# Order within a step: transposes ahead of the values of the job two back, high halves ahead of the outputs

## The chip, the cores and the metric

The kernel runs on one core of one Trainium2 chip. The metric is the device time of one execution in microseconds (us), on that one core. A core has a matrix engine (TensorE, PE in the profile, with its weight loads as PEld), VectorE (DVE), ScalarE (ACT), GpSimd (POOL) and a queue that issues DMAs (SyncE, SP). Each engine works through its own list of instructions in the order in which it was written. Engines wait for each other only by semaphores.

## The reference, cut to what matters

The input x is 4 sequences of 1024 rows of 1024 numbers. The block is a causal attention with 16 heads of 64 over a context, followed by one linear layer. Both have a layer norm ahead and a residual behind.

```
def attention(q, k, v):                      # per head, D = 64, SCALE = D ** -0.5
    scores = einsum('qd,kd->qk', q, k) * SCALE
    scores = where(key > query, -inf, scores)
    p = exp(scores - scores.max(-1))
    return (p / p.sum(-1)) @ v

x = x + attention(layernorm(x), ctx, ctx)
weight = einsum('oin,n->oi', sigmoid(pweight) - sigmoid(nweight), exps * sigmoid(mask_weight)) * scale
bias = bit_ste(einsum('on,n->o', pbias - nbias, bexps)) * biasscale
x = x + layernorm(x) @ weight.T + bias
```

## The kernel before, in words

The 4096 rows are 32 **tiles** of 128 rows, eight to a sequence. Tile t is number i = t mod 8 in its sequence and sees i + 1 blocks of 128 keys. The heads of a tile are cut into **jobs**: four heads to a job at i = 0 and 1, two at i = 2 and 3, one at i = 4 to 7. A tile so has 4, 4, 8, 8, 16, 16, 16 and 16 jobs, 352 in all. One job is one **step** of the main loop on every engine. A job with heads x (i + 1) blocks has 4 to 8 blocks.

What happens to job j, and where:

- **Scores** (PE, lines 395 to 419): queries times keys in two fp16 terms, and the causal mask as one more matmul, into `slot`, a PSUM buffer with two places (one per parity of j). They are issued in step j - 2, and wait until the exponentials of job j - 2 have freed the place.
- **Maxima** (DVE, line 647) and **exponentials** (ACT, line 533, each followed by a short read of the row sums), also in step j - 2. They leave the probabilities in fp32 in `p32`.
- **Transposes** (PE, line 427), step j: each block of probabilities is transposed in fp32 into `ptb`, a PSUM buffer with two places of four blocks. A job of 5 to 8 blocks fills both places, as chunk 0 and chunk 1. A chunk waits until the low half of the chunk two back has been taken from its place (`lo_done`, line 425).
- **High halves** (ACT, line 549), step j: each chunk is scaled and copied as fp16 to `pt`, after `t_done` of the chunk. Ahead of the first chunk ACT waits for `pv_done` of job j - 2 (line 546), since those values read the same place of `pt`.
- **Low halves** (DVE, line 653), step j: fp32 minus the high half, as fp16.
- **Values** (PE, lines 431 to 450), issued two steps later, in step j + 2: transposed probabilities times values, into `oacc`, the one PSUM buffer for the outputs of a group of four heads. The first job of a group waits until the output of the group before has been taken (`osb_done`).
- **Output** (ACT, line 556): when the values of a group's last job are done, ACT copies `oacc` to `osb`, in the step in which those values run. POOL adds it to the residual.

In the tiles of 8 and 16 steps, jobs q = 3, 6, 9, ... of tile 4 and later (92 jobs) are **turned by DMA** instead: ACT copies the high half of the untransposed probabilities (line 542), DVE makes the low half (line 661), and a DMA transposes both (`pd<-pd`, line 318). Such a job has no transposes, high halves or low halves in its own step. It has values, which wait for the DMA (`pt_in`).

The **linear** layer of an earlier tile is spread over the steps (line 464): 3 matmuls per step in a 16-step tile, 6 in an 8-step tile, 12 in a 4-step tile. The conversions of queries, context and y (lines 565, 573, 580) go at fixed steps. In a 16-step tile they stand at the end of steps 8, 4 and 0 on ACT. In the first 16 steps of the kernel the weights are also made (lines 488, 589, 594, 714, 718 and 885), and in the steps of jobs 4 and 5 the bias (`bias_part`). The linear layer of the last three tiles runs after the last job.

The order of the work is written out by hand in the loop of each engine (line 506 for PE, 616 for ACT, 772 for DVE). A step of PE was: scores of j + 2, values of j - 2, transposes of j, [weights, bias], linear. A step of ACT was: output, high halves of j, exponentials of j + 2 and the copy of a turned job, conversions. A step of DVE is: maxima of j + 2, low half of the turned job j + 1, reciprocals, low halves of j.

## Time and profile before

| what | value |
|---|---|
| median of 3 runs | 1213.82 us (1211.16 to 1218.65) |
| the profiled execution's own time | 1213.7 us |
| its span in the trace | 1211.9 us |
| busy PE, PEld | 1109.8 us, 803.6 us |
| busy DVE, ACT, POOL | 968.1 us, 922.2 us, 687.4 us |
| granted TensorE clock, mean | 0.982 |

Busy time is the sum of an engine's instructions. Matmuls overlap in the pipeline, so the length of one matmul's row is more than the time from its start to the next start. The length of a stage on PE is therefore read from the start of its first matmul to the start of the next stage's first matmul. The time that an engine stood idle ahead of an instruction stands in brackets behind the row, with what ended it.

### The profile page before, as it was taken

The numbers are of one execution on the slowest core, as the hardware profiler recorded it, in microseconds if no ns is written. First come the engines' busy times: TensorE is split into PE (matmuls) and PEld (weight loads), VectorE is DVE, ScalarE is ACT, GpSimd is POOL, SyncE is SP. The second block draws the span as 40 slices with busy tenths as digits, with TensorE's granted clock in tenths as the row PEclk, the third lists the DMA queues.
The fourth block names the chain that finished last, engine by engine and source line by source line (L and its number), as shares of the span: only waits on it lengthen the run. The fifth ranks groups of instructions, "written<-read, shape, count | busy, mean of one in ns | idle before, by whom it ended". The sixth has DMA issues, their size and how long they took to land. (4 is left out here: it accounts for less than half of the span.)

```text
span 1211.9 us, 28076 instructions
## 1 busy us (share of the span) xinstructions
PE 1109.8 (92%) x10788; PEld 803.6 (66%) x10788; DVE 968.1 (80%) x1424; ACT 922.2 (76%) x1898; POOL 687.4 (57%) x766
## 2 busy tenths in 40 slices
PE   4787889899999999889999999999999999899988
PEld 3676756566666776666766777676776676677753
DVE  5756677888888887888888887888888788888862
ACT  6899866688787787677787787788788787787750
POOL 3465546554446886454446986555348986463251
PEclk8889898999999999999999999999999999999999
DMA  9999726575759786675759886764658986654442
GB/s 317 287 321 330 256 71 118 129 148 108 150 121 175 178 186 130 140 141 106 151 120 201 150 191 128 159 158 107 127 119 199 183 173 143 135 105 97 86 88 70
DMA packets 382581, 190.88 MB, mean 158 GB/s; under 512 B 358128, under 2 KB 358128, under 8 KB 378352
## 3 DMA queue, kind: packets, MB, share of 16 engines
q1 hardware_dynamic: 381440, 189.05, 68.1%
q8 instruction: 86, 1.41, 0.5%
q14 instruction: 47, 0.39, 0.1%
q10 hardware_dynamic: 1008, 0.04, 0.1%
HBM read 67.15 MB, written 16.78 MB: 69 GB/s over the span
## 5 line engine op out<-in xcount | busy, mean ns | idle before, releaser
L533 ACT ACTIVATE p<-slot,mx 128x512 f32<-128x512 f32 (+7 forms) x512 | 378.0, 748 | 142.8 <-DVE mx L647 89.9
L647 DVE TENSOR_REDUCE mx<-slot 128x1 f32<-128x640 f32 (+7 forms) x352 | 356.8, 1016 | 32.4 <-PE slot L417 30.5
L464 PE MATMUL ffnb<-wt,yt 128*128 128x512 f16 x1464 | 373.0, 381 | 3.1 <-DVE ring L709 1.7
L653 DVE SCALAR_TENSOR_TENSOR pt<-ptb,pt 128x512 f16<-128x512 f32 (+1 forms) x504 | 281.9, 599 | 102.7 <-ACT pt L549 102.3
L413 PE MATMUL slot<-kt,qt 128*128 128x128 f16 (+3 forms) x1056 | 268.6, 284 | 16.4 <-ACT p L533 10.9
L414 PE MATMUL slot<-kt,qs 128*128 128x128 f16 (+3 forms) x1056 | 268.2, 284 | 0.0
L549 ACT ACTIVATE pt<-ptb 128x512 f16<-128x512 f32 (+1 forms) x504 | 239.9, 528 | 30.4 <-PE ptb L427 28.1
L427 PE MATMUL ptb<-id,p 128*128 128x128 f32 x1700 | 241.1, 280 | 12.2 <-DVE pt L653 10.4
L870 POOL TENSOR_TENSOR att<-osb 128x256 f32<-128x256 f32 x128 | 97.9, 765 | 271.0 <-ACT osb L556 266.4
L464 PEld LDWEIGHTS ffnb<-wt,yt 128*128 128x128 f16 x1464 | 136.9, 98 | 103.1 <-DVE ring L709 2.8
L446 PE MATMUL oacc<-v,pt 128*128 128x128 f16 x1700 | 180.3, 221 | 24.9 <-ACT osb L556 10.6
L427 PEld LDWEIGHTS ptb<-id,p 128*128 128x128 f32 x1700 | 182.5, 141 | 19.4 <-issue 16.8
L446 PEld LDWEIGHTS oacc<-v,pt 128*128 128x128 f16 x1700 | 150.1, 98 | 46.1 <-ACT osb L556 18.2
L448 PE MATMUL oacc<-v,pt 128*128 128x64 f16 x1700 | 172.9, 193 | 0.0
L413 PEld LDWEIGHTS slot<-kt,qt 128*128 128x128 f16 x1056 | 103.4, 98 | 93.7 <-ACT p L533 32.6
L661 DVE SCALAR_TENSOR_TENSOR pd<-p,pd 128x640 f16<-128x640 f32 (+3 forms) x92 | 135.4, 1472 | 17.0 <-ACT pd L542 14.5
L448 PEld LDWEIGHTS oacc<-v,pt 128*128 128x128 f16 x1700 | 148.0, 98 | 0.1
L414 PEld LDWEIGHTS slot<-kt,qs 128*128 128x128 f16 x1056 | 103.8, 98 | 53.6 <-issue 0.8
L417 PE MATMUL slot<-maskb,idb 128*128 128x128 bf16 x512 | 111.1, 221 | 0.0
L556 ACT ACTIVATE osb<-oacc 128x512 f32<-128x512 f32 x128 | 76.7, 599 | 42.8 <-PE oacc L448 42.7
L879 POOL TENSOR_TENSOR ring<-ring,att 128x256 f32<-128x256 f32 x128 | 102.5, 801 | 10.1
L533 ACT ACTIVATION_READ_ACCUMULATOR p<-slot,mx 128x1 f32 x512 | 108.1, 211 | 0.0
(90 smaller groups left out, 1451.1 us busy)
## 6 DMA issues: line engine op xcount, KB each, us to landing
ring<-in_x_dram SPq DMA_DIRECT2D x32, 512.0 KB, 4.3
cin<-in_ctx_dram SPq DMA_DIRECT2D x32, 512.0 KB, 4.6
out_dram<-ring SPq DMA_DIRECT2D x32, 512.0 KB, 3.4
qs<-qt SPq DMA_DIRECT2D x124, 128.0 KB, 2.9
v<-in_weights_dram SPq DMA_DIRECT2D x11, 1024.0 KB, 7.2
kt<-in_weights_dram SPq DMA_DIRECT2D x11, 1024.0 KB, 7.9
pd<-in_weights_dram SPq DMA_DIRECT2D x5, 1024.0 KB, 6.9
yt<-in_weights_dram SPq DMA_DIRECT2D x5, 1024.0 KB, 8.6
```

What stands on the lines that cost most here:

```text
L413: pe.matmul(dst, qt[:, t % 2, h, :], keys, start=True, stop=False, skip_group_check=True)
L414: last = pe.matmul(dst, qs[:, h, :], keys, start=False, stop=end <= i, skip_group_check=True)
L417: last = pe.matmul(slot[:, j.par, base + i * P:base + (i + 1) * P], idb[:, :], maskb[:, :], start=False, stop=True, skip_group_check=True)
L427: last = pe.transpose(ptb[:, c % 2, at * P:(at + 1) * P], p32[:, j.par, k * P:(k + 1) * P], id32[:, :])
L446: pe.matmul(oacc[:, h % GROUP, :], turned[:, k, :], v, start=blk == 0, stop=False, skip_group_check=True)
L448: last = pe.matmul(oacc[:, h % GROUP, 0:D], turned[:, j.blocks + k, :], v[:, 0:D], start=False, stop=blk == j.i, skip_group_check=True)
L464: last = pe.matmul(dst, yt[:, k % 2, a * KT_N + kk, :], wt[:, c, kk, half * 512:half * 512 + 512], start=r == 0, stop=r == 3 * KT_N - 1)
L533: last = nc.scalar.activation(p32[:, j.par, hh * j.keys:(hh + 1) * j.keys], slot[:, j.par, base:base + j.keys], ACT.Exp, bias=mx[:, j.par, ...
L549: nc.scalar.activation(pt[:, j.par, blocks.start:blocks.stop, :], ptb[:, c % 2, 0:P * len(blocks)].rearrange("p (k c) -> p k c", c=P), ACT ...
L647: nc.vector.tensor_reduce(mx[:, j.par, 0:j.heads], src[:, 0:j.heads, 0:j.keys], AX_X, ALU.max, negate=True).then_inc(mx_ready, 1)
L653: nc.vector.scalar_tensor_tensor(pt[:, j.par, j.blocks + blocks.start:j.blocks + blocks.stop, :], ptb[:, c % 2, 0:P * len(blocks)].rearran ...
L661: nc.vector.scalar_tensor_tensor(p16[:, size:2 * size], p32[:, j.par, 0:size], P_SCALE, p16[:, 0:size], ALU.mult, ALU.subtract).then_inc(p ...
```

## The change

Two calls are moved within the loop of one step, one on PE and one on ACT. No instruction is added or removed, and no wait is. DVE, POOL and SP keep their lists.

```diff
@@ -506,9 +506,9 @@
             for j in JOBS:
                 if j.n + 2 < len(JOBS):
                     scores(JOBS[j.n + 2])
+                transpose_p(j)
                 if j.n > 1:
                     values(JOBS[j.n - 2])
-                transpose_p(j)
                 if j.n < UNITS:
                     weights(j.n)
...
@@ -619,9 +619,9 @@
                     weights_high(j.n - 1)
                 if j.n - 1 in BIAS_JOBS:
                     bias_part(j.n - 1 - BIAS_JOBS[0])
+                high_parts(j)
                 if j.n > 1 and JOBS[j.n - 2].closes_group:
                     output(JOBS[j.n - 2].group)
-                high_parts(j)
                 if j.n + 1 < UNITS:
                     chunk_tanh(2 * j.n + 2)
```

The list of PE at the end of a step in the last tile (eight blocks), before. L464 is the linear layer, L413 to L417 the scores, L446 and L448 the values, L427 the transposes:

```order
L417 MATMUL slot<-maskb,idb 128x128
L446 MATMUL oacc<-v,pt 128x128
L448 MATMUL oacc<-v,pt 128x64
...
L427 MATMUL ptb<-id,p 128x128 x8
L464 MATMUL ffnb<-wt,yt 128x512 x3
```

and now:

```order
L417 MATMUL slot<-maskb,idb 128x128
L427 MATMUL ptb<-id,p 128x128 x8
L446 MATMUL oacc<-v,pt 128x128
L448 MATMUL oacc<-v,pt 128x64
...
L464 MATMUL ffnb<-wt,yt 128x512 x3
```

The sixteen matmuls of the values now stand between the transposes and the linear layer. In the step of a turned job there are no transposes, and its list is the same as before.

The list of ACT in step 13 of the last tile, with the step's neighbours, before. L556 is the output, L549 the high halves, L533 the exponentials (of job 15 behind the high halves), L542 the copy of that turned job, L580 a conversion of y:

```order
L533 ACTIVATE p,rowsum<-slot,mx 128x1024 x2
L556 ACTIVATE osb<-oacc 128x512
L549 ACTIVATE pt<-ptb 128x512 x2
L533 ACTIVATE p,rowsum<-slot,mx 128x1024
L542 ACTIVATE pd<-p 128x1024
L580 CAST y<-norm 128x1024
```

and now:

```order
L533 ACTIVATE p,rowsum<-slot,mx 128x1024 x2
L549 ACTIVATE pt<-ptb 128x512 x2
L556 ACTIVATE osb<-oacc 128x512
L533 ACTIVATE p,rowsum<-slot,mx 128x1024
L542 ACTIVATE pd<-p 128x1024
L580 CAST y<-norm 128x1024
```

The output changed places with both high halves. The exponentials stand behind both, as they did. A step has an output when job j - 2 closes a group of four heads: every step at i = 0 and 1, every second step at i = 2 and 3, and steps 1, 5, 9 and 13 of a 16-step tile.

## Rows read from the trace of the kernel before

**Rows 1.** The page, part 1: busy time, share of the span, instructions.

```profile
PE 1109.8 (92%) x10788; PEld 803.6 (66%) x10788; DVE 968.1 (80%) x1424; ACT 922.2 (76%) x1898; POOL 687.4 (57%) x766
```

**Rows 2.** Waits of PE: waiting tile, releaser, us in total, times, longest.

```profile
PE oacc L446 <- DMA pd<-pd: 11.0, 10, 2.4
PE oacc L446 <- ACT osb L556: 10.6, 20, 0.9
PE ptb L427 <- DVE pt L653: 10.4, 21, 2.0
PE oacc L446 <- DVE pt L653: 9.4, 14, 1.3
PE oacc L446 <- issue: 4.1, 2, 2.1
```

**Rows 3.** Timeline, tile 31 (i = 7), steps 10 and 11: start, length, instruction, count.

```profile
1156.55 1.09 ACT L549 ACTIVATE pt<-ptb 128x512 f16<-128x512 f32 x2 [0.17 <-PE ptb L427]
1157.17 1.29 DVE L653 SCALAR_TENSOR_TENSOR pt<-ptb,pt 128x512 f16<-128x512 f32 x2 [0.61 <-ACT pt L549]
...
1158.29 0.22 PE L446 MATMUL oacc<-v,pd 128*128 128x128 f16 x1
...
1158.97 1.07 PE L427 MATMUL ptb<-id,p 128*128 128x128 f32 x8
...
1159.88 0.81 PE L464 MATMUL ffnb<-wt,yt 128*128 128x512 f16 x3
...
1160.53 0.33 PE L413 MATMUL slot<-kt,qt 128*128 128x384 f16 x1
...
1161.45 0.22 PE L446 MATMUL oacc<-v,pt 128*128 128x128 f16 x1
```

**Rows 4.** Timeline, tile 29 (i = 5), steps 1 to 3, by engine.

```profile
1043.85 0.59 ACT L556 ACTIVATE osb<-oacc 128x512 f32<-128x512 f32 x1
1044.34 0.86 ACT L549 ACTIVATE pt<-ptb 128x384 f16<-128x384 f32 x2
...
1044.85 1.02 DVE L653 SCALAR_TENSOR_TENSOR pt<-ptb,pt 128x384 f16<-128x384 f32 x2 [1.87 <-ACT pt L549]
...
1045.56 0.92 PE L427 MATMUL ptb<-id,p 128*128 128x128 f32 x6 [0.38 <-DVE pt L653]
1046.32 0.81 PE L464 MATMUL ffnb<-wt,yt 128*128 128x512 f16 x3
1046.96 0.33 PE L413 MATMUL slot<-kt,qt 128*128 128x384 f16 x1
...
1047.68 0.22 PE L446 MATMUL oacc<-v,pt 128*128 128x128 f16 x1
```

**Rows 5.** Timeline, tile 29 (i = 5), steps 5 to 7, by engine.

```profile
1053.62 1.01 DVE L653 SCALAR_TENSOR_TENSOR pt<-ptb,pt 128x384 f16<-128x384 f32 x2
...
1055.51 1.03 ACT L573 CAST v<-cin 128x1024 f16<-128x1024 f32 x1
1056.44 0.59 ACT L556 ACTIVATE osb<-oacc 128x512 f32<-128x512 f32 x1
1056.93 0.86 ACT L549 ACTIVATE pt<-ptb 128x384 f16<-128x384 f32 x2
1057.67 0.91 ACT L533 ACTIVATE p<-slot,mx 128x768 f32<-128x768 f32 x1
...
1054.31 0.92 PE L427 MATMUL ptb<-id,p 128*128 128x128 f32 x6
...
1057.09 0.23 PE L446 MATMUL oacc<-v,pt 128*128 128x128 f16 x1 [0.50 <-ACT osb L556]
...
1058.73 0.34 PE L413 MATMUL slot<-kt,qt 128*128 128x384 f16 x1 [0.31 <-ACT p L533]
```

**Rows 6.** Timeline, tile 31, steps 13 and after, to the last values.

```profile
1164.38 1.07 PE L427 MATMUL ptb<-id,p 128*128 128x128 f32 x8
...
1165.11 1.08 ACT L549 ACTIVATE pt<-ptb 128x512 f16<-128x512 f32 x2
```

## The prediction

> **What bounds the kernel now.** I read the page's busy times first, then the waits of PE, then its timeline step by step. PE is busy 92% of the span, DVE 80%, ACT 76% [rows 1], and from tile 12 on the slices of the page show PE at nine tenths with the clock fully granted. So the bound is PE's own list. The reader should see in the waits how little is left to win. The values wait for an output 10.6 us in 20 places, for low halves 9.4 us in 14, for the turning DMA 11.0 us in 10, and 4.1 us in the two steps of the bias; the transposes wait for low halves 10.4 us in 21 [rows 2]. Everything else that the change touches is slack, and the timeline tells how much of it there is. That is where this prediction is decided: the change costs PE no instruction, it only moves the moments at which PE releases ACT and at which PE needs DVE.
>
> **Part 1: transposes ahead of values.** I take a step of eight blocks. From the starts of its stages on PE, the transposes take 0.91 us (1158.97 to 1159.88), linear 0.65, scores 0.92 (1160.53 to 1161.45), and values 0.68 (1158.29 to 1158.97) [rows 3]. A transpose is thus 0.114 us, and one chunk of four 0.455.
>
> What ACT waits for: the high halves of j need both the first chunk transposed and the values of j - 2. Before, the values came first, and ACT started when the first chunk was ready, while PE turned the second. Now ACT starts when the values are done, and these come last. The high halves start later by the second chunk, 0.46 us, less or more by what ACT had in front.
>
> What PE waits for: the transposes of j + 1 need the low halves of j, for the places of `ptb`. Before, linear, scores and values stood between. Now only linear and scores do. So the loop high half, low half, next transposes is tightened from both ends.
>
> I price it for two neighbouring steps that both have transposes, from the end of the values' slot on PE. The results land some 0.15 us later (a row of 0.22 us against a distance of some 0.06 to the next start). An engine wakes in 0.06 us: the output ends at 1057.03, the values start at 1057.09 [rows 5]. The low half starts 0.62 us after the high half, and two take 1.29 [rows 3]. The transposes start about 0.15 us after the low half that frees their place [rows 4]: start 1044.85, half of the pair and its overlap to about 1045.40, PE at 1045.56. Sum to the second chunk: 0.15 + 0.06 + 0.62 + 1.29 + 0.15 = 2.27 us. PE gets there after linear, scores and the first chunk: 0.65 + 0.92 + 0.455 = 2.03. PE waits 0.24 us. For six blocks the same sum goes 0.15 + 0.06 + 0.51 + 1.02 + 0.15 = 1.89 against 0.64 + 0.72 + 0.34 = 1.70 [rows 4]: 0.19 us. Before, the values in between (0.68) and the earlier start of ACT (0.46) left about 0.9 us of slack in the first case.
>
> How often: a 16-step tile turns jobs 3, 6, 9, 12 and 15 by DMA, and then DVE has two steps. The pairs left are (0,1), (1,2), (4,5), (7,8), (10,11) and (13,14). The first two stand in the head of the tile, where ACT and DVE set the pace anyway. In tile 29, at step 2, the chain is output at 1043.85, high halves at 1044.34, low halves at 1044.85, transposes at 1045.56 after 0.38 of idling, linear at 1046.32 [rows 4]. With the high halves first, all of that chain but the output moves 0.49 earlier. The second chunk is then through at about 1045.8, the values wait for the output, which by then is done, and take 0.51: linear starts at 1046.3. Nothing gained, nothing lost. Pair (4,5) goes into part 2. Three free pairs a tile remain, in 16 tiles, half of them with 0.19 and half with 0.24 (I take i = 4 like 5, and 6 like 7): 3 x (8 x 0.19 + 8 x 0.24) = **+10.3 us**. Tiles of 4 and 8 steps have 12 and 6 linear matmuls in the step, so at least 0.65 us more between values and transposes: no wait there, 0.
>
> What it wins: where the values wait for a DMA and the step has transposes, these now run inside the wait. Ten such waits hold 11.0 us, the longest of 2.4 is that of the last job, where no transposes are left [rows 2]. Of the other 8.6 us in nine waits each can lose at most its transposes, 0.58 to 0.91, which makes some 4.7; ACT starts the chain to the DMA up to 0.46 later, which takes back a third: **-3 us** (bounds 0 and -4.7). In the two bias steps of 4.1 us the transposes fit in the wait too, but these are steps in which ACT with its tanh is behind; two other steps of the start, where ACT waits for the first chunk, lose as much: 0 (bounds -1.5 and +1).
>
> **Part 2: output behind the high halves.** The dear case is step 5 of a 16-step tile. ACT is late there with a conversion of the context (1055.51), then comes the output (1056.44), the high halves (1056.93) and the exponentials (1057.67); the values of the next group, in step 6, wait 0.50 for the output and start at 1057.09; and step 6 is that of a turned job, with no transposes to fill the gap [rows 5]. Now the high halves go first, 0.74 us, the output starts at 1057.18 and ends at 1057.77, the values start at 1057.83. The exponentials stay where they are, so the scores of step 7, which waited 0.31 for them, lose that cover first: values and linear take 1.15, 1057.83 + 1.15 = 1058.98 against 1058.73: +0.25 us. In step 5 itself the transposes wait for the low halves of 1053.62 either way, and the values now come behind them [rows 5]; the 0.51 that this costs is hidden by ACT's conversion. 16 tiles x 0.25 = **+4.0 us**. In all other steps the group's next values have linear, scores and transposes between, and the output is 0.3 us or more ahead.
>
> The trace so shows high halves and transposes as two sides of one buffer: at 1156.55 ACT takes the first chunk while PE still turns the second [rows 3]. The Trainium skill has this as a rule (Perfetto Trace Analysis, section Matmuls): independent matmul groups should rotate through PSUM banks, so that the evacuation of one overlaps the next group. It speaks against the change, which makes ACT start only when both places of `ptb` are full. If every one of the 11 steps with transposes of a 16-step tile lost that overlap of 0.35 to 0.46, the sum would be 16 x 11 x 0.4 = 70 us; I hold the row's slack of 0.9 us against it, and take only what exceeds it.
>
> **Part 3: the end.** In step 13 of the last tile the transposes and values together end at 1165.29 on PE in either order. ACT began its high halves at 1165.11 [rows 6]; now at 1165.29 + 0.15 + 0.06 = 1165.50, and with high halves (0.97) and output (0.49) ahead, the exponentials of the last job start at about 1166.96, against 1166.08, which is 1165.11 + 0.97. Its copy, low half, DMA and values follow in one chain, on which PE then waits 2.4 us [rows 2]: **+0.9 us**.
>
> **Sum.** 10.3 + 4.0 - 3 + 0.9 = +12.2 us on the profiled execution's own 1213.7 us: 1225.9, taken as 1226. The median of the runs shown is 1213.82, so the same sum applies. A change of 1% is 12 us, about what a measurement can tell from no change.
>
> **The rivals.**
>
> *Slack holds, about no change.* The pair waits rest on sums of five terms with lags of 0.06 to 0.15; if each lag is 0.05 less they shrink to almost nothing, and the 0.25 of part 2 can be taken back in the head of the next tile, where DVE sets the pace. For it: PE idles little now, and waits of such tiles absorb small shifts. Against it: 1.89 against 1.70 has the low halves at their shortest. Time: 10.3 to 2, 4 to 2, so +2: 1216. Chance 0.33.
>
> *Faster: the waits ahead of the values vanish.* The transposes cover the output waits of step 2 (8 of them, 5 us), the DMA waits (4.7), the bias (4.1) and, at step 4, the first chunk starts while DVE makes the second low half (14 x 0.35 = 5): -19, 1195. Against it: the output itself goes later, and after step 4 PE waits for the exponentials, so what is won there is given back. The Trainium skill argues this way (Perfetto Trace Analysis, section Optimization Strategy): find the gaps on the engine that bounds, and make what blocks it start sooner. The rows show that the change starts nothing sooner, it only puts other work in the gap. Chance 0.08.
>
> *Clearly slower: ACT's start decides everywhere.* With an output behind the high halves and the whole behind the values, the exponentials of j + 2 start 0.9 us later in the steps with an output, as in part 3. Where the slack of the scores of j + 4 is under 0.9, PE waits. If half of the 64 steps with an output in 16-step tiles pay 0.5, that adds 16, and the pairs at the tile heads add 2 x 16 x 0.2 = 6: +34, 1248. It decides from the point where ACT has less than 0.5 us to spare in a step with a conversion. Against it: in a step of eight blocks, 0.65 + 0.92 + 0.91 + 0.68 + 0.65 = 3.8 us lie between values and those scores, against 0.2 + 0.97 + 0.49 + 1.3 = 3.0 for ACT. Chance 0.13.
>
> The forecast has 0.46. Its own range, with the bounds above, is 1218 to 1236, half of it above the 1% mark. **Numbers:** 1226, range 1209 to 1241 (left out: most of the faster case, half of the clearly slower one). Faster by over 1%: 0.08. Within 1%: 0.33 and somewhat under half of 0.46, less a little of the forecast's middle: 0.48. Slower: 0.44.
>
> **What would show it.** New waits of PE at line 427 for line 653 in steps 8, 11 and 14 of the 16-step tiles, 0.1 to 0.3 us each, 48 of them. The output wait at step 6 grows from 0.5 to about 1.2, and the wait for exponentials behind it goes. The DMA waits shrink to some 6 us. ACT's waits for transposes (L549 for L427) turn into waits for values. A tile of 16 steps gets 0.8 to 1 us longer, tiles of 4 and 8 steps stay. The prediction is wrong if the 8-step tiles move, if the pair steps show no wait, or if the scores wait for exponentials in steps 2, 10 or 14.

## The result, and the profile after

The changed kernel takes 1221.12 us (median of 11 runs, 1216.54 to 1225.27) where the kernel before took 1213.82 (11 runs beside them). The ratio is 1.006, with a 95% interval of 1.0042 to 1.0079. The forecast was 1226, so the sign is right, and the size is three fifths of it: 7.3 us of 12.2. The profiled execution has a span of 1219.3 us and a clock of 0.985.

Part 1 of the page, changed kernel:

```profile
PE 1104.2 (91%) x10788; PEld 798.1 (65%) x10788; DVE 973.6 (80%) x1424; ACT 924.2 (76%) x1898; POOL 700.0 (57%) x766
```

The work is that of [rows 1], and the counts are equal. PE is busy 5.6 us less and the span is 7.4 longer, so PE idles more. POOL is busy 12.6 us longer with the same 766 instructions. Of these, 8.3 are one group, the split of y (L856), which comes back below.

The waits of PE, changed kernel:

```profile
PE ptb L427 <- DVE pt L653: 39.6, 58, 3.1
PE oacc L446 <- ACT osb L556: 12.2, 19, 1.1
PE slot L413 <- ACT p L533: 7.1, 8, 5.0
PE oacc L446 <- issue: 5.2, 2, 3.0
PE oacc L446 <- DMA pd<-pd: 4.0, 4, 2.3
PE oacc L446 <- DVE pt L653: 1.4, 1, 1.4
```

Against [rows 2]: the transposes' wait for low halves went from 10.4 us in 21 places to 39.6 in 58. The values' wait for low halves went from 9.4 to 1.4, and their wait for the turning DMA from 11.0 to 4.0. One wait was traded for another.

The waits of ACT, changed kernel. Before, its row for L549 was a wait for the transposes, `PE ptb L427`, of 28.1 us in 45 places:

```profile
ACT pt L549 <- PE oacc L448: 85.6, 86, 3.0
```

The high halves now wait for the end of the values, as the prediction said. Here is the stretch of [rows 3], tile 31, steps 10 and 11:

```profile
1163.17 1.09 ACT L549 ACTIVATE pt<-ptb 128x512 f16<-128x512 f32 x2 [0.38 <-PE oacc L448]
...
1163.62 0.33 PE L413 MATMUL slot<-kt,qt 128*128 128x384 f16 x1
...
1163.80 1.29 DVE L653 SCALAR_TENSOR_TENSOR pt<-ptb,pt 128x512 f16<-128x512 f32 x2 [0.96 <-ACT pt L549]
...
1164.64 1.16 PE L427 MATMUL ptb<-id,p 128*128 128x128 f32 x8
...
1165.63 0.22 PE L446 MATMUL oacc<-v,pd 128*128 128x128 f16 x1
...
1166.96 0.33 PE L413 MATMUL slot<-kt,qt 128*128 128x384 f16 x1
```

From the start of the scores to that of the transposes there are 1.02 us, against 0.92 without a wait, and the transposes take 0.99 against 0.91. The step lasts 3.34 us (1163.62 to 1166.96). The same step lasted 3.16 before.

Steps are compared below as times on PE from the start of one step's scores to the start of the next step's, in us. "Both" is the change, and "held" is the version whose POOL waits (explained with its experiment, as is "places"). A star marks a turned job's step, and the headings give the blocks of a job:

```
tile, step      before  both  PE only  ACT only  places  before held  both held
23 (8)  1        3.08   4.31    3.67     3.51     4.31      3.07        4.30
23 (8)  2        3.47   3.35    3.83     3.94     3.29      3.48        3.35
23 (8)  4        3.87   3.13    3.22     3.16     3.13      3.17        3.13
23 (8)  5        3.57   3.76    4.25     3.16     3.76      3.21        3.76
23 (8)  6*       3.49   3.05    2.80     3.55     3.05      3.49        3.06
23 (8)  8        3.16   3.35    3.34     3.16     3.13      3.16        3.35
23 (8) 11        3.16   3.35    3.34     3.16     3.13      3.16        3.35
23 (8) 13        3.42   3.64    3.64     3.42     3.15      3.44        3.65
23 (8) 14        3.43   3.63    4.12     3.71     3.63      3.43        3.62
29 (6)  1        2.98   3.51    3.14     2.96     3.49      2.94        3.51
29 (6)  2        3.84   3.43    3.93     3.99     3.45      3.85        3.43
29 (6)  4        3.74   2.53    3.23     2.55     2.53      2.56        2.53
29 (6)  5        3.15   3.52    3.65     2.86     3.53      2.63        3.51
29 (6)  6*       3.01   2.79    2.50     3.30     2.79      3.02        2.79
29 (6)  8        2.56   2.69    2.70     2.56     2.53      2.56        2.70
29 (6) 11        2.56   2.79    2.69     2.61     2.98      2.56        2.80
29 (6) 14        2.66   2.69    3.18     2.69     2.64      3.68        2.70
18 (6, 8 steps) 1 3.43  4.23    4.07     3.43     4.22
18 (6, 8 steps) 6* 2.79 3.12    2.79     2.79     3.13
```

Steps 8 and 11 are what the prediction was mostly about, and they came nearly as it said (0.19 us at eight blocks, where it had 0.24). Two rows it did not have are larger. Step 1 costs 1.2 us at eight blocks and 0.8 in an 8-step tile. Step 4 gains 0.7 and 1.2 us, although nothing in the sum gained there.

Step 13 of tile 23 gets 0.22 us longer. At its end lies a wait that the prediction named as a sign of being wrong: the scores at the start of step 14 wait for exponentials. Tiles 7, 15 and 22 have it too, with 0.35 to 0.38 us, and the kernel before shows no such wait over 0.1 us there. (The 3.68 us in step 14 of tile 29 hold a wait of the values of 0.85 us for the turning DMA.)

```profile
904.96 0.23 PE L413 MATMUL slot<-kt,qt 128*128 128x128 f16 x1 [0.35 <-ACT p L533]
```

The output case of step 5, tile 29, changed kernel (against [rows 5]):

```profile
1060.22 1.03 ACT L573 CAST v<-cin 128x1024 f16<-128x1024 f32 x1
1061.16 0.86 ACT L549 ACTIVATE pt<-ptb 128x384 f16<-128x384 f32 x2
1061.91 0.60 ACT L556 ACTIVATE osb<-oacc 128x512 f32<-128x512 f32 x1
1062.38 0.91 ACT L533 ACTIVATE p<-slot,mx 128x768 f32<-128x768 f32 x1
```

```profile
1062.56 0.23 PE L446 MATMUL oacc<-v,pt 128*128 128x128 f16 x1 [0.74 <-ACT osb L556]
...
1063.73 0.33 PE L413 MATMUL slot<-kt,qt 128*128 128x384 f16 x1
```

The wait for the output has grown from 0.50 to 0.74, where the forecast had about 1.2, and the scores behind have no wait for exponentials any more, as forecast.

The last exponentials of the kernel, changed kernel (against [rows 6], where high halves at 1165.11 led to exponentials at 1166.08):

```profile
1171.90 1.08 ACT L549 ACTIVATE pt<-ptb 128x512 f16<-128x512 f32 x2 [0.58 <-PE oacc L448]
1172.87 0.60 ACT L556 ACTIVATE osb<-oacc 128x512 f32<-128x512 f32 x1
1173.34 1.13 ACT L533 ACTIVATE p<-slot,mx 128x1024 f32<-128x1024 f32 x1
```

From high halves to exponentials there are 1.44 us, against 0.97. From the start of the last scores to these exponentials it is 4.13 against 3.30: +0.83, where part 3 had +0.9.

### The profile page after: what moved, and what is told of

It reads as the page before. It is cut to its first block, busy times and chain, and to the rows that moved or that the text cites. A ratio compares the mean times of both kernels' runs of the same rounds, so it can differ in the third digit from the quotient of the medians.

```text
span 1219.3 us, 28076 instructions
## 1 busy us (share of the span) xinstructions
PE 1104.2 (91%) x10788; PEld 798.1 (65%) x10788; DVE 973.6 (80%) x1424; ACT 924.2 (76%) x1898; POOL 700.0 (57%) x766
## 4 chain that ended last, share of the span: by engine, by line
PE 33%; DVE 21%; ACT 16%; issue 12%; POOL 9%; DMA 6%; SPq 2%; POOLq 0%; ACTq 0%; DVEq 0%
PE ffnb L464 8%; PE ptb L427 6%; DVE pd L661 6%; DVE pt L653 5%; DMA pd<-pd 5%; ACT pt L549 4%; PE oacc L446 4%; DVE mx L647 4%; ACT p L533 4%; DVE stats L674 3%; PE slot L413 3%; PE slot L414 3%; ACT pd L542 3%; PE ffnb L488 3%; POOL norm L828 2%
## 5 line engine op out<-in xcount | busy, mean ns | idle before, releaser
L533 ACT ACTIVATE p<-slot,mx 128x512 f32<-128x512 f32 (+7 forms) x512 | 378.3, 749 | 129.5 <-DVE mx L647 64.0
L464 PE MATMUL ffnb<-wt,yt 128*128 128x512 f16 x1464 | 372.4, 381 | 3.9 <-DVE ring L709 3.1
L653 DVE SCALAR_TENSOR_TENSOR pt<-ptb,pt 128x512 f16<-128x512 f32 (+1 forms) x504 | 281.6, 599 | 90.4 <-ACT pt L549 89.3
L549 ACT ACTIVATE pt<-ptb 128x512 f16<-128x512 f32 (+1 forms) x504 | 239.6, 526 | 90.8 <-PE oacc L448 85.6
L413 PE MATMUL slot<-kt,qt 128*128 128x128 f16 (+3 forms) x1056 | 268.4, 284 | 12.8 <-ACT p L533 7.1
L870 POOL TENSOR_TENSOR att<-osb 128x256 f32<-128x256 f32 x128 | 105.1, 821 | 296.9 <-ACT osb L556 296.9
L427 PE MATMUL ptb<-id,p 128*128 128x128 f32 x1700 | 237.9, 278 | 40.1 <-DVE pt L653 39.6
L427 PEld LDWEIGHTS ptb<-id,p 128*128 128x128 f32 x1700 | 181.0, 141 | 74.1 <-issue 61.2
L446 PE MATMUL oacc<-v,pt 128*128 128x128 f16 x1700 | 180.2, 220 | 18.9 <-ACT osb L556 12.2
L464 PEld LDWEIGHTS ffnb<-wt,yt 128*128 128x128 f16 x1464 | 120.6, 98 | 100.9 <-DVE ring L709 3.7
L448 PE MATMUL oacc<-v,pt 128*128 128x64 f16 x1700 | 173.1, 193 | 0.0
L446 PEld LDWEIGHTS oacc<-v,pt 128*128 128x128 f16 x1700 | 151.0, 98 | 28.2 <-ACT osb L556 17.3
L413 PEld LDWEIGHTS slot<-kt,qt 128*128 128x128 f16 x1056 | 103.8, 98 | 80.7 <-ACT p L533 16.8
L448 PEld LDWEIGHTS oacc<-v,pt 128*128 128x128 f16 x1700 | 148.1, 98 | 2.0
L417 PE MATMUL slot<-maskb,idb 128*128 128x128 bf16 x512 | 111.2, 221 | 0.0
L533 ACT ACTIVATION_READ_ACCUMULATOR p<-slot,mx 128x1 f32 x512 | 108.9, 213 | 0.0
L879 POOL TENSOR_TENSOR ring<-ring,att 128x256 f32<-128x256 f32 x128 | 100.9, 788 | 10.0
L674 DVE BATCH_NORM_STATS2 stats<-ring 128x6 f32<-128x512 f32 x128 | 81.6, 678 | 17.6 <-DMA ring<-in_x_dram 10.6
```

The lines of the kernel that those rows point to most:

```text
L413: pe.matmul(dst, qt[:, t % 2, h, :], keys, start=True, stop=False, skip_group_check=True)
L427: last = pe.transpose(ptb[:, c % 2, at * P:(at + 1) * P], p32[:, j.par, k * P:(k + 1) * P], id32[:, :])
L446: pe.matmul(oacc[:, h % GROUP, :], turned[:, k, :], v, start=blk == 0, stop=False, skip_group_check=True)
L448: last = pe.matmul(oacc[:, h % GROUP, 0:D], turned[:, j.blocks + k, :], v[:, 0:D], start=False, stop=blk == j.i, skip_group_check=True)
L464: last = pe.matmul(dst, yt[:, k % 2, a * KT_N + kk, :], wt[:, c, kk, half * 512:half * 512 + 512], start=r == 0, stop=r == 3 * KT_N - 1)
L533: last = nc.scalar.activation(p32[:, j.par, hh * j.keys:(hh + 1) * j.keys], slot[:, j.par, base:base + j.keys], ACT.Exp, bias=mx[:, j.par, ...
```

## The experiments

Each ratio is that of its runs to runs of the kernel before on the same chip, with its 95% interval. Medians: PE only 1230.31 us, ACT only 1215.51, third place 1204.15, places by count 1212.08, that with step 1 old 1211.38, output first in step 5 1197.26, POOL waits 1198.44, all together 1194.5, change with POOL waiting 1220.15, that with step 1 old 1223.09, step 13's output first 1218.89, steps 13 to 15 old 1213.52. The kernel before took 1213.34 to 1215.29 beside them. Of each run one execution was traced, and the first four tiles alone take from 156 to 164 us in these traces, so a difference of two spans is not sure to 3 us or so. The steps of the later tiles repeat much more closely.

**Each half alone.** PE's order (first diff) and ACT's (second), each against the kernel before:

```diff
+                transpose_p(j)
                 if j.n > 1:
                     values(JOBS[j.n - 2])
-                transpose_p(j)
```

> Only PE's order is changed (transposes ahead of values); ACT keeps the output ahead of the high halves. Theory A, the loop through the two places of the transpose buffer: all of the loss at steps 8, 11 and 14 (0.19 us each at eight blocks) and at step 1 (0.5 to 1.2 us) is from PE's order, so it stays: 1.005 to 1.008 times before. At step 1 the output is now ahead, so the high halves start 0.5 us later there and the transposes of step 2 wait longer. Theory B, the output is what costs (it holds up the values of step 6): then this kernel is at 1.000 to 1.002, and step 6 of the 8-block heads-of-two tiles is back from 3.2 to 2.6 us. Both say that step 6 goes back; they part on the total.

```diff
+                high_parts(j)
                 if j.n > 1 and JOBS[j.n - 2].closes_group:
                     output(JOBS[j.n - 2].group)
-                high_parts(j)
```

> Only ACT's order is changed (high halves ahead of the output); PE keeps values ahead of transposes. Theory A: steps 8, 11, 14 and 1 as before; what is left is step 6, where the values wait 0.6 to 0.8 us for the output, and at step 2 the values wait longer for it: 1.000 to 1.003. Theory B: the whole of the loss is here, 1.005 to 1.008.

Measured: PE only 1.013 (1.011 to 1.0149), ACT only 1.0007 (0.9995 to 1.0019), and both 1.006. The first wait of PE in each, PE only ahead:

```profile
PE ptb L427 <- DVE pt L653: 50.4, 72, 3.1
```

```profile
PE oacc L446 <- ACT osb L556: 38.3, 39, 2.2
```

PE only is dearer than either theory had it (at most 1.008), and the halves do not add up. PE's half carries all of the pair waits (steps 8 and 11: 3.34 against 3.35 with both). With the output still ahead of the high halves, its steps 5 and 14 at eight blocks are dearer yet, by 0.5 us each. ACT's half turns slack ahead of the values into a wait for the output, and still comes out even. The table says where that is paid back: in step 4.

**Does ACT's start decide the pair waits?** In the pairs ACT waits for the values of j - 2 only since they read the same place of `pt`. With a third place that wait goes. The place lies where the bias was, and this kernel leaves the bias out of its result.

```diff
-                reached(act, pv_done, j.n - 1)
+                reached(act, pv_done, j.n - 1 if j.n < 10 else j.n - 2)
...
-                    nc.scalar.activation(pt[:, j.par, blocks.start:blocks.stop, :],
+                    nc.scalar.activation(pt_of(j)[:, blocks.start:blocks.stop, :],
```

> The changed kernel with three places for the transposed probabilities in place of two, so that the high halves of j wait for the values of j - 3, long done, and can start when the first chunk is transposed. The third place takes the room of the bias; the bias addition reads another tensor, so the bias is left out of the result, with the same instructions. If the loop is tightened from both ends, as predicted, giving back ACT's start (0.35 to 0.46 us earlier) takes away the waits of steps 8, 11 and 14 (3.35 back to 3.16 us at eight blocks, 48 steps, about 8 us in all) and much of step 14's wait for exponentials; step 1 keeps most of its loss if DVE's moments and maxima set it. Total 0.996 to 1.001 times before. If only PE's need for the low halves matters and not ACT's start, steps 8, 11 and 14 stay at 3.35 and the total at 1.006.

Measured: 0.9924 (0.9896 to 0.9952), under both theories' numbers. Turned jobs do not write `pt`, so the same can be had in most steps without new memory, by giving the two places in turn to the jobs that need one:

```diff
+UNTURNED = [j for j in JOBS if j.d is None]
+for _k, _j in enumerate(UNTURNED):
+    _j.place = _k % 2
+    _j.free = UNTURNED[_k - 2].n + 1 if _k > 1 else 0
...
-                reached(act, pv_done, j.n - 1)
+                reached(act, pv_done, j.free if j.d is None else j.n - 1)
```

> The changed kernel, with the two places of the transposed probabilities given out by a count of the jobs that PE transposes, and not by the job's parity. Since the turned jobs use neither, the high halves of job 4 then wait for the values of job 1, of 5 for 2, of 7 for 4, of 8 for 5, all done before the step begins; only in step 2 do they still wait for values of the same step. Nothing is left out. Theory A (loop through the transpose buffer, with ACT's start as one end of it): steps 8, 11 and 13 go back to 3.13 us at eight blocks as with three places, steps 1 and 2 stay: 0.997 to 1.001 times before, that is 0.6% under the changed kernel. Rival: what the kernel with a third place gained came from its start or from the room of the bias; then this one stays at 1.004 to 1.006.

Measured: 0.9978 (0.9962 to 0.9993). PE's and ACT's waits in this kernel (its lines are four higher):

```profile
PE ptb L431 <- DVE pt L657: 36.6, 66, 3.1
```

```profile
ACT pt L553 <- PE oacc L452: 44.5, 37, 3.1
```

ACT's wait for the values halves, and steps 8 and 11 of tile 23 go from 3.35 back to 3.13 in both kernels, the time of steps 7 and 10, which have no wait. Step 8 does so in every 16-step tile. So the loop of part 1 is shown there: the late start of ACT is one end of it, and without it these pairs cost nothing. It does not hold of every pair. Step 14 of tile 23 keeps its 3.63, and step 11 of tile 29 gets longer, 2.98 against 2.79. PE's wait for low halves as a whole only falls from 39.6 to 36.6 us, since most of it lies in steps 1, 2 and 5. Step 1 of tile 23 keeps 4.31 in both. It is another mechanism.

The third place measured 0.5% under the places by count. From tile 4 to tile 30 the two take the same (934.8 and 935.1 us). Most of the difference of their spans, 2.2 of 3.1 us, lies in the first four tiles, and no run tells what it is from.

**The head, first attempt.** Is it that step 1's transposes need the low halves of job 0, which DVE makes behind the ring update, the moments and the maxima?

```diff
-                transpose_p(j)
+                ahead = not (j.q == 1 and steps(j.t) > 4)
+                if ahead:
+                    transpose_p(j)
                 if j.n > 1:
                     values(JOBS[j.n - 2])
+                if not ahead:
+                    transpose_p(j)
```

> As the kernel with places by count, but in step 1 of the 8- and 16-step tiles PE keeps the old order (values, then transposes). If the transposes of step 1 wait for low halves that DVE makes only after the moments and the maxima, the values behind them are held up for nothing: step 1 goes from 4.31 back to 3.1 at eight blocks and from 4.23 to 3.4 in the 8-step tiles, but the steps to 4, where ACT and DVE set the pace, take half of it back: 0.992 to 0.998. Rival, the chain of ACT and DVE alone sets the sum of steps 1 to 4: then the sum does not move and the total is that of places by count, within 0.2%.

Measured, on top of the places by count: 0.9972 (0.9956 to 0.9987), no difference from 0.9978. The same edit on top of the change with POOL waiting (below):

> The changed kernel with POOL held back (1.0057), and PE's old order in step 1 alone of the 8- and 16-step tiles. It prices the one step that the prediction took for free: there the transposes wait for low halves that DVE makes behind a result, the moments and the maxima. If step 1 carries the loss, steps 1 to 4 lose about 1.0 us in a tile of eight blocks and 0.8 us in one of heads-of-two with six blocks, less at five and six blocks in the long tiles: 0.994 to 0.999 times before. If the head of a tile is set by ACT and DVE, as the prediction had it, the total stays at 1.004 to 1.007.

Measured: 1.0066 (1.0043 to 1.009) against 1.0057. My theory fell. Step 1 of tile 23 came down from 4.30 to 3.71, and step 2 went up from 3.35 to 3.89. The sum of steps 1 to 4 stayed at 12.98 against 13.03. The wait moved by one step, as the rival said.

**The output in step 5.** The output ahead of the high halves again, where the next job is turned, on top of the places by count. Of the steps with an output that is step 5 alone, in tiles of 8 and 16 steps:

```diff
-                high_parts(j)
+                late = JOBS[min(j.n + 1, len(JOBS) - 1)].d is None
+                if late:
+                    high_parts(j)
                 if j.n > 1 and JOBS[j.n - 2].closes_group:
                     output(JOBS[j.n - 2].group)
+                if not late:
+                    high_parts(j)
```

> As the kernel with places by count, but ACT takes the output ahead of the high halves where the next job is a turned one (step 5 of the 8- and 16-step tiles), as before the change. Part 2 of the prediction says that the late output costs 0.25 us per 16-step tile in steps 5 to 7, and the trace of the changed kernel shows 0.5 us at step 6 of the 8-step tiles: -4 - 6 x 0.6 = -7 us, 0.6% under places by count. Rival, the exponentials behind high halves and output set the pace: steps 5 to 7 keep their sum in the 16-step tiles and only the 8-step tiles gain, -3 us.

Measured: 0.9858 (0.9833 to 0.9883), 1.2% under the places by count, which is more than I gave it. Step 6 falls from 3.05 to 2.81 in tile 23, from 2.79 to 2.50 in tile 29, from 3.13 to 2.79 in tile 18, and by 0.6 in the 8-step tiles of i = 3. Over 22 tiles these are some 7 us. The rest lies in single steps of some tiles (step 11 of tile 29 from 2.98 to 2.53, step 1 of tile 7 from 4.32 to 3.59). The turned low halves are shorter too (x92, mean 1432 ns against 1563), which is the term of the next experiment. How the rest divides, I did not separate.

**Where step 4's gain comes from.** The low half of turned job 3 reads two tensors in SBUF, and POOL's split of y (L856) reads SBUF beside it. Kernel before, tile 29, POOL and then DVE:

```profile
1046.70 2.13 POOL L856 TENSOR_TENSOR y<-norm,y 128x1024 f16<-128x1024 f32 x1
```

```profile
1046.99 2.65 DVE L661 SCALAR_TENSOR_TENSOR pd<-p,pd 128x768 f16<-128x768 f32 x1 [0.25 <-ACT pd L542]
```

Changed kernel, the same two, with the POOL instruction ahead of them:

```profile
1052.82 0.73 POOL L879 TENSOR_TENSOR ring<-ring,att 128x256 f32<-128x256 f32 x1
...
1053.03 1.33 DVE L661 SCALAR_TENSOR_TENSOR pd<-p,pd 128x768 f16<-128x768 f32 x1 [0.74 <-ACT pd L542]
...
1053.50 2.86 POOL L856 TENSOR_TENSOR y<-norm,y 128x1024 f16<-128x1024 f32 x1
```

The same DVE instruction takes 2.65 us if POOL's split started 0.29 us ahead of it, and 1.33 if it was itself 0.47 ahead of the split, with only the last half microsecond of L879 in its way. Then POOL's split takes 2.86 in place of 2.13. To test it, the kernel **before** got one wait and nothing else: POOL's split in step 2 waits for that low half.

```diff
                     for k in y_at(t, s, 2):
+                        if steps(t) == 16:
+                            pool.wait_ge(p16_lo, JOBS[FIRST[t] + 3].d + 1)
                         y_split(k)
```

> The kernel before, untouched on PE and ACT, but in step 2 of the 16-step tiles POOL's split of y waits until DVE has made the low half of turned job 3. Theory C: the 0.9 to 1.3 us that step 4 gained in both kernels with the output behind the high halves is not from their order as such, but from POOL starting its split (2.13 us) after DVE's low half and not before it, since then DVE takes 1.33 us for it and not 2.65. Then step 4 goes from 3.75 to about 2.6 us at six blocks, with PE and ACT as before, and the total is 0.992 to 0.997. Rival: the order on ACT and PE shortens step 4 itself; then step 4 stays at 3.7 and the total at 1.000 or above, with POOL 1 us later.

Measured: 0.9868 (0.9844 to 0.9891). An added wait makes the kernel 1.3% faster, which is more than the theory gave it. DVE and then POOL in tile 29 of this kernel:

```profile
1036.86 0.96 DVE L661 SCALAR_TENSOR_TENSOR pd<-p,pd 128x768 f16<-128x768 f32 x1 [0.25 <-ACT pd L542]
```

```profile
1037.89 2.13 POOL L856 TENSOR_TENSOR y<-norm,y 128x1024 f16<-128x1024 f32 x1 [1.28 <-DVE pd L661]
```

Both are now at their shortest. Step 4 of tile 29 falls from 3.74 to 2.56, the same 1.2 us that the change gained (2.53), with PE's and ACT's orders as before. So that gain is no merit of the new orders. Over tiles 4 to 30, step 4 of the 16-step tiles gives 10.6 us here and 11.0 in the change. Step 5 gives another 4.7 here (3.15 to 2.63 in tile 29), which the change does not show. With the output late, POOL adds it later, starts its split later, and DVE gets in first. The groups by line show it (mean ns of one behind the busy time) in the kernel before, in the changed one, and in this one:

```profile
L856 POOL TENSOR_TENSOR y<-norm,y 128x1024 f16<-128x1024 f32 x23 | 51.6, 2242 | 0.0
```

```profile
L856 POOL TENSOR_TENSOR y<-norm,y 128x1024 f16<-128x1024 f32 x23 | 59.9, 2606 | 0.4 <-ACT y L580 0.4
```

```profile
L856 POOL TENSOR_TENSOR y<-norm,y 128x1024 f16<-128x1024 f32 x23 | 49.0, 2131 | 24.0 <-DVE pd L661 24.0
```

**The change at an equal port.** The same wait on top of the change:

> The changed kernel with POOL held back as in the kernel that had PE and ACT untouched. In the changed kernel DVE was already first at the port for job 3, so nothing is left to win there: 1.002 to 1.006 times before. The distance to the kernel with the same wait and the old orders (0.987) is then the price of the two moved calls once POOL's place at the port is equal on both sides: 1.6 to 2%, some 20 us. If instead the wait helps here as much as it did there (0.990 to 0.995), the gain of step 4 in the changed kernel was not the port.

Measured: 1.0057 (1.0037 to 1.0078). The change had that gain already, so the wait gives it nothing. Against the kernel before with the same wait (0.9868) the two moved calls cost 1.9%, a quotient of two ratios, each measured beside the kernel before. By the spans it is 1218.1 - 1198.7 = 19.4 us.

**The head, second attempt.** In the kernel before, tile 23, DVE came to the ring update 0.34 us after the scores of step 0 had started on PE (857.57):

```profile
857.91 0.68 DVE L709 TENSOR_TENSOR ring<-ffnb,ring 128x512 f32<-128x512 f32 x1
```

In the changed kernel it is 1.17 us (scores at 860.96), and PE pays in step 1 (the last row shows five of its eight transposes):

```profile
862.13 0.68 DVE L709 TENSOR_TENSOR ring<-ffnb,ring 128x512 f32<-128x512 f32 x1
...
865.25 1.28 DVE L653 SCALAR_TENSOR_TENSOR pt<-ptb,pt 128x512 f16<-128x512 f32 x2
```

```profile
866.08 0.84 PE L427 MATMUL ptb<-id,p 128*128 128x128 f32 x5 [0.98 <-DVE pt L653]
```

DVE enters the tile late, so the cause can lie in the tile ahead. Two kernels put back the old order there, on top of the change with POOL waiting: ACT's in step 13, and then PE's in steps 13 to 15 as well.

```diff
+                late = j.q != 13
+                if late:
+                    high_parts(j)
                 if j.n > 1 and JOBS[j.n - 2].closes_group:
                     output(JOBS[j.n - 2].group)
+                if not late:
+                    high_parts(j)
```

> The change with POOL's y split held back behind the low half of turned job 3, and ACT's old order (output ahead of the high halves) in step 13 of the 16-step tiles alone. With POOL held back and the change whole the time was 1.0057 of the kernel before. Theory: the 1.0 us that steps 1 and 2 of an eight-block tile lose comes in from the tile ahead. VectorE enters the head late: in tile 23 its ring update (L709) starts 1.17 us after the scores of job 2 (step 0), against 0.34 in the kernel before, because in step 13 the exponentials of the turned job 15 stand behind high halves and output. Then step 13's old order gives back the scores' wait of step 14 (0.36) and about 0.5 us of the head, in the eight tiles of seven and eight blocks and little elsewhere: 7 us, ratio 1.000. Rival: the head is slow by its own steps 0 and 1, and step 13 has only its own 0.36: 3 us, ratio 1.003, the head unchanged.

```diff
+                ahead = j.q < 13
+                if ahead:
+                    transpose_p(j)
                 if j.n > 1:
                     values(JOBS[j.n - 2])
+                if not ahead:
+                    transpose_p(j)
```

> As e14, and besides PE's old order (values ahead of transposes) in steps 13 to 15 of the 16-step tiles. Theory: now VectorE enters the head of the next tile as early as in the kernel before, so that step 1 no longer waits 1.0 us for the low halves of job 0: about 1 us a tile back in the eight tiles of seven and eight blocks, plus the 0.2 of the pair (13, 14) in all sixteen: ratio 0.994 to 0.997 against 1.0057. Rival: the head keeps its 1.0 us and only the pair's 0.2 and the wait for exponentials in step 14 come back: ratio 1.000.

Measured: 1.0044 (1.0025 to 1.0062), and 0.9998 (0.9982 to 1.0014). The first can't be told from 1.0057. Step 1 of tiles 15 and 23 does fall (4.31 and 4.30 to 3.66), but step 14 rises by 0.5 (3.63 to 4.12) and step 15 falls by 0.3, and the tiles of i = 4 get longer, so most of the gain is taken back. The second is 0.6% better, at the rival's number, but not as the rival said. The head does improve: in tile 15 step 1 goes from 4.31 to 3.48 and step 14 from 3.63 to 3.44, in tile 22 step 1 goes from 4.23 to 3.66, while in tile 23 it stays at 4.25.

Tile 23 is no exception to the theory, since DVE still comes late there. At eight blocks, with PE's new order in step 1, the step's length follows the delay of the ring update behind the scores of step 0:

```
kernel, tile                      delay   step 1
steps 13 to 15 old, tile 15        0.34    3.48
step 13's output first, tile 23    0.52    3.66
steps 13 to 15 old, tile 23        1.11    4.25
change with POOL waiting, tile 23  1.17    4.30
```

Each time step 1 takes 3.14 us and the delay, to 0.01. In the kernel before it takes 3.07 with a delay of 0.34. So of the 1.24 us that step 1 costs at eight blocks, 0.83 are DVE's later entry, brought in from steps 13 to 15 of the tile ahead, and 0.41 are PE's order in the step itself. Why DVE still enters tile 23 late when tile 15 is cured is left open.

**All together.** Places by count, output first in step 5, step 1's transposes behind the values, and POOL's wait:

> The parts that won, together: places by count, output ahead of the high halves where the next job is a turned one, transposes ahead of values everywhere but in step 1 of the 8- and 16-step tiles, and POOL's split of y in the 16-step tiles behind DVE's low half of job 3. The old order of step 1 gained nothing in the kernel with places by count. If that was because the output and so POOL's split came early again and took the port first, then with POOL held back the 0.9 to 1.0 us a tile is free now: 0.974 to 0.982 times before. If the sum of steps 1 to 4 is set by ACT and DVE in any case, it stays at 0.984 to 0.987.

Measured: 0.9847 (0.9817 to 0.9877). It beats both kernels by 1.5% and more. Steps 1 to 4 of tile 23 take 12.97 us, as in the change (13.04), so the port was not what kept step 1's old order from gaining. But the one wait of POOL in the kernel before has 0.9868, and the intervals overlap. Whether the two new orders, repaired, add anything to it is not shown.

## Why the prediction was right in sign, and what its size owes to luck

The kernel before loses 13.2 us of its span if POOL waits (1211.9 to 1198.7). From there the change costs 19.4 (to 1218.1), and 1.2 more without the wait (1219.3): -13.2 + 19.4 + 1.2 = +7.4. Such a sum of spans comes out by construction, and its terms are sure to 3 us or so. The prediction's +12.2 was for the moved calls alone; it stands against 19.4, and the port's 13 us were not in it at all. Two errors of opposite sign brought the total near, and that was luck.

Where the 19.4 lie, from the lengths of the steps with POOL held: in the 16-step tiles up to tile 30, +6.7 in steps 1 to 4, +6.2 in steps 5 and 6, +3.9 in steps 8, 11 and 14 (net of two DMA waits of the values that were shorter, 2.6 us), +1.0 in step 13 and -1.6 in the others. The 8-step tiles from tile 10 on have +3.9, the 4-step tiles -0.3, and tile 31 with what follows it +2.5. The first four tiles were 3.0 shorter, which is within what they vary by.

- **Part 1, the pair waits: the mechanism right, the size a little high.** Predicted 0.24 and 0.19 us a pair in steps 8, 11 and 14. Measured 0.19 in steps 8 and 11 at eight blocks, 0.14 and 0.23 in tile 29, and in step 14 0.2 down to nothing at six blocks. That is about 0.4 x 16 for the first two and some 1.5 for the third: 8 us against 10.3, before what shorter DMA waits give back in the same steps. The third place and the places by count take the waits of step 8 away in all tiles, and that of step 11 at eight blocks, but not that of step 14 there. A wait of the scores for exponentials, which the prediction named as a sign of being wrong and put at nothing, came at step 14 in four tiles of seven and eight blocks: 1.4 us in all.
- **"Nothing gained, nothing lost" at the head: the step that failed.** It was worked out at tile 29 and holds there: with POOL held, steps 1 and 2 take 6.79 us before and 6.94 after. I carried it over to all tiles. At eight blocks steps 1 to 4 lose 1.0 us (12.00 to 13.03), and at seven 0.7 (11.80 to 12.53). The working looked at the chain of output and high halves. At eight blocks the chain that decides is DVE's: step 1 takes 3.14 us and DVE's delay, and the delay went from 0.34 to 1.17 us. In tile 15 all of that growth goes with the old orders in steps 13 to 15 of the tile ahead, which the working did not look at; in tile 23 it stays, and why is open.
- **Tiles of 8 steps, predicted 0.** The three of i = 2 take 82.67 us together, against 79.36, and the three of i = 3 take 85.45, against 84.03: +4.7 us. Step 1 pays 0.8 in tile 18, step 4 pays 0.4 (the linear layer waits 0.47 for DVE's ring update), and step 6 pays 0.33 there and 0.6 at i = 3. With the output first in step 5, step 6 has all of that back. The prediction named this as a sign of being wrong. The linear layer's 0.65 us cover does hold at steps 2, 5 and 7, but not at the head (step 1's transposes wait 0.56 us for low halves in tile 18), and an 8-step tile has a turned job 6 behind an output as a 16-step one has.
- **Part 2, the output: right place, somewhat undersized.** With POOL held, steps 5 and 6 together go from 6.70 to 6.82 at eight blocks, from 6.16 to 6.50 at seven, and from 5.65 to 6.30 in tile 29: 0.1 to 0.65, about 0.4 x 16 = 6 against 4.0. "The 0.51 that this costs is hidden by ACT's conversion" is what failed. The transposes of step 5 in tile 29 wait 0.73 for the low halves of job 4, a pair like the others, behind which ACT's conversion and the output come later too. "Either way" was not so: with the old orders and POOL held, tile 29's step 5 takes 2.63 us, and 3.51 with the new ones.
- **The DMA waits.** They fell by 7.0 us to 4.0, where the forecast had them at some 6. In part the transposes cover them, as said; in part, as I read it, PE now waits ahead of the transposes, while the DMA runs anyway. That 7 us is no gain of 7 us in time.
- **Part 3, the end:** +0.83 against +0.9.
- **What was missing: the port.** Nothing in the sum had a DVE instruction that changes its length. The rows that would have told it were in the trace of before: among the 92 low halves of turned jobs, those of six blocks take 0.96 us for job 6 of tile 29 and 2.65 for job 3, and those of seven blocks in tile 22 take 1.09 and 2.47. Rows that differ by a factor of two at one shape, while another engine has a row that starts just ahead, are the sign of a collision. What moves either engine's start then moves the time.
- **The Trainium skill's rule of rotating PSUM banks** (Perfetto Trace Analysis, section Matmuls) pointed in the right direction, and the 70 us that it would have made if every overlap were lost did not come: with POOL held the cost was 19.4. The slack of 0.9 us took most of it, as held against it. The rival "faster" said that step 4 would win; step 4 did win, more than it said, but through the port and not since the first chunk starts earlier.

## What to carry to other kernels

Putting a producer's work ahead of other work on the engine that bounds shortens one distance in a ring of buffers as it lengthens another. Add up the whole ring (producer, copy, second copy, next producer) at the tightest size, and do it again where a tile begins, since slack worked out in one tile does not hold in another. Before costing a reordering, list the instructions whose length varies at one shape and name their partner: the port between VectorE and GpSimd gave 1.3% here, by a single added wait, while neither order of the change gained anything over the kernel before (1.013 and 1.0007).

## What the runs showed of the hardware

I had not expected that one VectorE instruction varies from 0.96 to 2.65 us by what GpSimd started a moment before. The low half of a turned job (`SCALAR_TENSOR_TENSOR`, both inputs in SBUF, 128 x 768) takes 0.96 us with POOL idle. In the kernel before, tile 29, it starts 1.84 us ahead of the end of POOL's split (1046.70 + 2.13 - 1046.99) and takes 1.69 longer. In the changed kernel it starts 0.52 us ahead of the end of L879 (1052.82 + 0.73 - 1053.03) and takes 0.37 longer. The split behind it starts 0.86 us ahead of the low half's end (1053.03 + 1.33 - 1053.50) and takes 0.73 longer (2.86 for 2.13). So each time the later one is longer by what was left of the earlier one, but for some 0.15 us, and the split that was ahead keeps its 2.13. The Trainium skill states this (SBUF — State Buffer, section Who interferes with whom): a VectorE instruction with two SBUF inputs contends with a GpSimd instruction that reads SBUF, the contention is an exclusive lock of the port pair that both share, and the order of issue decides which of them is blocked. The trace agrees, by these three numbers. The ports themselves no trace shows. The low halves that read PSUM (L653) do not show it: one of four blocks takes 0.68 us before and after.

It strikes in other places too. In tile 22, POOL's split of q (L845) and the low half of turned job 12 (128 x 896) start 0.08 us apart before, the low half first with 1.09 us, and 0.30 apart in the changed kernel, POOL first, and then the low half takes 2.78. PE pays it in step 13 of that tile: 3.79 us against 2.86. There the change had bad luck, as it had good luck in step 4. The 8-step tiles of i = 3 have it as well: the low half of job 3 (128 x 1024) takes 1.23 us before and 2.69 in the changed kernel.
